# Two tiles of values moved beside the first scores, the first shift transposed half a step sooner

## The reference

```python
Q = (x @ Wq.T + bq).reshape(B, S, H, hd).transpose(0, 2, 1, 3)
K = (x @ Wk.T + bk).reshape(B, S, H, hd).transpose(0, 2, 1, 3)
V = (x @ Wv.T + bv).reshape(B, S, H, hd).transpose(0, 2, 1, 3)
scores = jnp.einsum('bhqd,bhkd->bhqk', Q, K) / (TAU * np.sqrt(hd))
A = jax.nn.softmax(scores, axis=-1)
A_stable = LAMBDA_JUMP * A + (1.0 - LAMBDA_JUMP) * L[None, None, :, :]
out = jnp.einsum('bhqk,bhkd->bhqd', A_stable, V)
out = out.transpose(0, 2, 1, 3).reshape(B, S, D)
return out @ Wo.T + bo
```

## Time and profile before

| | us |
|---|---|
| median of 3 runs | 2013.65 |
| lowest and highest run | 2012.37, 2017.76 |
| the profiled execution | 2025.48 |
| its span from first to last instruction | 2023.7 |
| PE busy | 1972.7 (97%) |
| DVE busy | 1621.5 (80%) |
| ACT busy | 1374.0 (68%) |
| mean granted clock of PE | 0.989 |

### The profile page before, as it was taken

One profiled execution on the slowest core, in us unless ns is written; L12 is line 12 of the kernel. 1 busy time (PEld: TensorE's weight loads), 2 busy tenths in 40 slices (PEclk: granted clock), 3 DMA queues, 4 the chain that ended last, 5 costly groups with the idle time before them and its releaser, 6 DMA issues. The chain is left out here.

```text
span 2023.7 us, 48037 instructions
## 1 busy us (share of the span) xinstructions
PE 1972.7 (97%) x16480; PEld 1051.8 (52%) x16480; DVE 1621.5 (80%) x2035; ACT 1374.0 (68%) x2471; POOL 347.4 (17%) x379
## 2 busy tenths in 40 slices
PE   7999999999999999999999999999999899999997
PEld 4543333333333333333333333333687689999996
DVE  6779999999999999999999999994255565555554
ACT  3338888888888888888888888889544422222331
POOL 1370001000100010001000100010024532232233
PEclk9979999999999999999999999999999899999999
DMA  7935335433543355335533553341122777788884
GB/s 268 243 81 114 74 84 118 91 73 79 121 93 73 76 112 105 73 74 107 112 73 74 105 114 73 73 97 49 42 76 87 286 228 238 241 256 302 256 267 111
DMA packets 105849, 264.09 MB, mean 130 GB/s; under 512 B 20896, under 2 KB 52768, under 8 KB 99104
## 3 DMA queue, kind: packets, MB, share of 16 engines
q1 hardware_dynamic: 92624, 245.29, 45.2%
q0 software_dynamic: 13152, 17.83, 4.5%
HBM read 206.95 MB, written 73.94 MB: 139 GB/s over the span
## 5 line engine op out<-in xcount | busy, mean ns | idle before, releaser
L619 DVE TENSOR_REDUCE part_max<-psum 128x1 f32<-128x1024 f32 x1024 | 1241.9, 1222 | 59.5 <-PE psum L741 47.0
L674 ACT ACTIVATE probs<-psum 128x512 f32<-128x512 f32 x2048 | 1111.1, 596 | 153.2 <-PE psum L754 86.1
L754 PE MATMUL psum<-score_q,score_k 50*128 50x512 f32 x2048 | 749.5, 448 | 1.2 <-DMA score_q<-shift_row 1.2
L741 PE MATMUL psum<-max_k,max_q 48*128 48x512 f32 x2048 | 742.4, 451 | 1.2 <-DVE part_max L619 1.1
L766 PE MATMUL psum<-probs,v_ones 128*32 128x256 f32 x8192 | 658.0, 393 | 9.4 <-ACT heads_sb L689 9.0
L754 PEld LDWEIGHTS psum<-score_q,score_k 50*128 50x128 f32 x2048 | 308.6, 186 | 408.6 <-ACT probs L674 394.0
L766 PEld LDWEIGHTS psum<-probs,v_ones 128*32 128x32 f32 x8192 | 162.5, 108 | 383.3 <-issue 200.8
L741 PEld LDWEIGHTS psum<-max_k,max_q 48*128 48x128 f32 x2048 | 296.0, 186 | 13.9 <-issue 7.5
L1159 ACT ACTIVATE x_sb<-psum,x_sb 128x512 f32<-128x512 f32 (+1 forms) x160 | 101.4, 635 | 260.0 <-PE psum L1520 253.4
L1539 PE MATMUL psum<-w,h_hi 128*128 128x256 f32 x1120 | 204.9, 280 | 0.6 <-issue 0.3
L1539 PEld LDWEIGHTS psum<-w,h_hi 128*128 128x128 f32 x1120 | 180.0, 189 | 11.6 <-issue 0.5
(11 more groups left out here) (179 smaller groups left out, 1367.7 us busy)
## 6 DMA issues: line engine op xcount, KB each, us to landing
w<-w_split SPq DMA_DIRECT2D x40, 2048.0 KB
max_q<-qk_pieces SPq DMA_DIRECT2D x192, 128.0 KB, 7.4
score_k<-qk_pieces SPq DMA_DIRECT2D x192, 128.0 KB, 4.6
xs<-in_pads SPq DMA_DIRECT2D x33, 528.0 KB, 5.9
qk_pieces<-pieces SPq DMA_DIRECT2D x32, 512.0 KB, 4.7
w_split<-w_pair SPq DMA_DIRECT2D x32, 512.0 KB, 6.6
max_k<-qk_pieces SPq DMA_DIRECT2D x192, 64.0 KB, 7.4
score_q<-qk_pieces SPq DMA_DIRECT2D x192, 64.0 KB, 2.2
```

Of the source, the lines that this page charges most:

```text
L619: nc.vector.tensor_reduce(part_max[:, t, p:p + 1], ps_m[p].rearrange("q b f -> q (b f)"), axis=AXIS.X, op=ALU.max).then_inc(m_read, 1)
L674: nc.scalar.activation(probs[kb % 2][:, chunk * BLOCK:(chunk + 1) * BLOCK], bank_of(at), ACT.Exp, scale=float(HD) ** -0.5).then_inc(exp_do ...
L741: last = nc.tensor.matmul(ps_m[p][:, h, :], max_q[u][rows, t * P:(t + 1) * P], max_k[u][rows, p * BLOCK:(p + 1) * BLOCK], start=True, stop ...
L754: nc.tensor.matmul(bank_of(at), score_k[u][rows, kb * P:(kb + 1) * P], score_q[u][rows, part * BLOCK:(part + 1) * BLOCK], start=True, stop ...
```

## The change

Six edits, all in the lead-in of `attend`:

- `v_tiles_before` spreads 28 instead of 30 tiles over halves 0 to 36, and puts tile 30 behind the score of half 38 and tile 31 behind that of half 39.
- The last bank, 15, is `ps_o` instead of `ps_s[1]` (`ps_v`). PE doesn't wait for an earlier bank ahead of it.
- At half 38 PE waits for 15 copied banks instead of 16. A wait for all 16 stands behind the lead-in, ahead of the heads' loop.
- SHIFT_HALF is 34 instead of 35; BANKS_BEFORE_SHIFT follows from the two, 13 instead of 15.
- ACT copies bank 15 between the second and third exponential of the first key block.
- `copy_v` is told its bank.

```diff
-    SHIFT_HALF = 2 * (ST + 1) + 1
+    SHIFT_HALF = 2 * (ST + 1)
...
-        return V_AHEAD + half * (TILES - V_AHEAD) // (FIRST_SCORES - 1) if half < FIRST_SCORES else TILES
+        spread = V_AHEAD + half * (TILES - 2 - V_AHEAD) // (FIRST_SCORES - 1)
+        return spread if half < FIRST_SCORES else min(TILES, TILES - 2 + half - FIRST_SCORES)
...
+    ps_v = [ps_s[r % VB] for r in range(BANKS - 1)] + [ps_o]
...
-        for r in range(BANKS_BEFORE_SHIFT // VB * VB, BANKS):
+                copy_v(b, vb, ps_s[vb])
+        for r in range(BANKS_BEFORE_SHIFT // VB * VB, BANKS - 1):
...
-            copy_v(r // VB, r % VB)
+            copy_v(r // VB, r % VB, ps_v[r])
         for c in range(CH):
             exp(0, 0, c, False)
+            if c == 1:
+                copy_v((BANKS - 1) // VB, (BANKS - 1) % VB, ps_o)
...
-            if t == 0 and r >= VB:
+            if t == 0 and VB <= r < BANKS - 1:
                 pe.wait_ge(v_copied, r - VB + 1)
...
-                last = nc.tensor.matmul(ps_s[vb][:, t * DIM:(t + 1) * DIM], xnT[:, b, k, toks], w_v[:, k, :],
+                last = nc.tensor.matmul(ps_v[r][:, t * DIM:(t + 1) * DIM], xnT[:, b, k, toks], w_v[:, k, :],
...
-                    pe.wait_ge(v_copied, BANKS)
+                    pe.wait_ge(v_copied, BANKS - 1)
...
+        pe.wait_ge(v_copied, BANKS)
```

More of the change, by code:

```diff
@@ L689, in copy_o, with copy_v @@
             nc.scalar.activation(heads_sb[:], ps_o, ACT.Copy).then_inc(o_copied, 1)
-        def copy_v(b, vb):
+        def copy_v(b, vb, bank):
             act.wait_ge(v_ready, VB * b + vb + 1)
-            nc.scalar.activation(v_tiles(b, vb), ps_s[vb].rearrange("p (t h d) -> p t h d", t=2, d=HD), ACT.Copy
+            nc.scalar.activation(v_tiles(b, vb), bank.rearrange("p (t h d) -> p t h d", t=2, d=HD), ACT.Copy
                                  ).then_inc(v_copied, 1)
@@ L698, in _ @@
             for vb in range(VB):
-                copy_v(b, vb)
-        for r in range(BANKS_BEFORE_SHIFT // VB * VB, BANKS):
+                copy_v(b, vb, ps_s[vb])
+        for r in range(BANKS_BEFORE_SHIFT // VB * VB, BANKS - 1):
             if r == BANKS_BEFORE_SHIFT:
```

## The result

The changed kernel is slower: 2026.64 us median of 18 runs (lowest 2018.38), against 2014.28 for the kernel before in the same job (lowest 2012.37). The ratio is 1.0062, with a 95% interval of 1.0040 to 1.0083. In a second job it was 2027.7 against 2014.39, ratio 1.0063 (1.0036 to 1.0090). The forecast was 2011.75, within 2002 to 2016. The profiled execution took 2030.82 us, with a span of 2029.0. One execution of each kernel in the first job was disturbed (2745.67 and 2302.79 us) and is left out of the ratio; without the two the medians are 2025.59 and 2013.97.

A forecast was written before the change was run, and what follows sets the result against it. PE was taken to bound the kernel, busy 97% of the span; 1.8 us by the maxima and 2.0 by the values were taken as 1.9 off 2013.65, giving 2011.75 us, range 2002 to 2016.

The forecast's parts named there:

- Steps 1 and 2: Lead-in: two tiles fewer ahead of half 37 take 2.12 us off PE; the earlier shift removes PE's 1.19 us wait.
- Step 3: Scores to heads' loop: maxima 42 start at 129.35, 1.8 us sooner; first values matmuls come 2.0 us sooner.
- Step 4: Wait for bank 15 ahead of the heads' loop costs nothing, 0.7 us cover; GpSimd's later pass is hidden.
- Step 2: Shift half a step sooner: lands at 124.0, PE wants it at 124.6; SP's entries behind it about 4 us sooner.
- The sum: Whole change: 1.8 us by the maxima and 2.0 by the values, taken as 1.9; bounds 0.7 and 2.4.
- The main doubt: Behind the lead-in: the median run before may well lack the profiled execution's low-clock stretch, which cost 9.1 us.
- Rival B: Lead-in: filling the gap also keeps the clock up, 1.9 + 9.1 = 11.0 us off, 2002.7 us; chance 0.21.
- A: Lead-in: idle time is filled, the median run's clock unchanged, 1.9 us off, 2011.75 us; chance 0.60.
- Rival D: Clock falls in the changed median run, for instance behind DVE's starving at 128: 7.2 us slower, 2020.9; chance 0.07.
- What would show it: Profile signs: PE busy over 4.3 of 5 us in 124 to 129; wrong if clock 0.50 within 130 to 150.

The follow-up runs named there:

- sp_after: The changed kernel, with SP issuing in each head the loads of the maxima's operands ahead of the weight chunk's store: 2008.11 us, ratio 0.9950 to the kernel before.
- sp_before: The kernel before, with SP issuing in each head the loads of the maxima's operands ahead of the weight chunk's store: 2013.46 us, ratio 0.9988.
- sp_after_again: The same kernel as sp_after, run once more in another job beside the changed kernel: 2007.56 us, ratio 0.9955 to the kernel before.
- pool_late_before: The kernel before with three more copies of the router weight's high part on POOL ahead of its long pass: 2028.41 us, ratio 1.0041.

## Why the prediction was wrong, point by point

- Steps 1 and 2, tiles and shift: right as to PE. PE reached half 37 at 123.59 (123.8 forecast), the transpose stood at 118.66 (119.2), the wait of 1.19 is gone.
- Step 3: right to 0.1 us at maxima 42 and the first values, so the gain of some 1.9 at that point is there (1.74 and 2.23).
- **Step 4 failed.** It said that POOL's lateness is hidden, since "The next thing wanted of it is the split of the second shift, at 168.68 now". The lateness was sized nearly right: some 1.5 us forecast, 1.67 measured at the start of the pass. Step 4 even reckoned POOL's work behind the pass, the first chunk's split among it, to an end near 153.7 (153.92 measured), but did not ask who waits for that split. SP's store does, and behind that store stand loads for which PE waits. Step 2 looked down SP's queue behind the shift and stopped at the first chunk's load; its "Nothing of PE's waits for these" is true of the band, the pads and that load, but the store and, two entries behind it, the loads that count come next. The sum put both the wait and its clock at nothing; in the profiled execution they were 8.1 us of wait and 14.5 us of low clock. Step 4's other claim, that the wait for bank 15 costs nothing, held.
- The question that was not asked is one of slack: how much sooner may PE come before it meets the loads? In the profiled execution before, PE came at 167.63 and the loads landed near 163.6 (165.39 less 1.84), so the slack was some 4.1 us. The changed kernel brought PE there at 157.2, 10.4 us sooner (the gain of the lead-in, and the 9.1 us that the clock no longer cost), and the loads 1.84 later. Together that is 12.3 us taken from 4.1, which leaves a wait of 8.2 us, and 8.1 were measured; the sum must come out, since the landing is read from the changed kernel's own trace. What it shows is that most of the slack was used up by the better clock and not by POOL. So every us that PE gains ahead of these loads is paid back as waiting once the slack is gone. I had asked what the faster clock does to POOL's shift (157.7 against an end at 153.7) and did not ask it of the DMAs.
- The main doubt, whether the median run before has a low stretch, was well placed. The answer is a short one, by estimate: in three later jobs 45 of 97 executions of the kernel before show a clock of 0.993 or 0.994 at some 2013 us, which is about 24 us at the low clock, against 16 in `sp_after`. The profiled execution, with 20 us at the low clock right behind the lead-in, was not typical.
- Rival B named the right mechanism in the lead-in: filling the gap keeps the clock up. Of 5.35 us between `sp_before` and `sp_after`, 1.9 is step 3's; the rest, 3.4, fits the shorter low stretch of `sp_before`, which by its rows costs 8.8 x (1 - 50/86.5) = 3.7 us, with 86.5 for the matmuls of 8.8 us at full clock. So A (1.9) and B (11.0) each held a part of it, but the loads took all of it away again.
- Rival D had the sign and the half clock, but with DVE's starving at 128 as the cause, and the price as 7.2. The trace shows 1.00 through there. What brought the clock down was a gap of 8.1 us that no rival held.
- "What would show it" listed a low clock within 130 to 150 and no stretch behind it, so it would have found nothing there.

What stays open is why the low stretch lasts 8 to 33 us behind the gap in one profile and another, and by the clocks of the unprofiled executions up to some 70. How the loss divides between wait and clock in the median execution is an estimate: the changed kernel's medians lie 18.5 and 20.1 us above those of `sp_after` and `sp_after_again`; some 8.2 of it is the wait, the other 10 to 12 the clock.

## What to carry to other kernels

Work that an engine hands over later is priced by everyone who waits for it, and a queue of DMAs hands the wait on: follow each wait on it to the entries behind, until one is found that the critical engine needs. When the critical engine gets faster, ask of every load that is timed by another engine whether it still lands in time. Put the loads that the critical engine needs ahead of stores that wait for a side job; here that order, or an earlier side job, turned a change that lost 12 us by the medians into one that gains 7.

## What the runs showed of the hardware

- In the lead-in the granted clock fell behind a stretch in which no single idle time of PE was over 1.4 us. In all six profiles without the whole change it fell between 128 and 131; PE had been busy there 3.55 to 3.65 of the 5.00 us from 124 on. In all seven with the whole change, busy 4.63 to 4.94 us in the same stretch, it held. A gap does not always do it: at 1582 in the kernel before PE was busy 0.63 of 2 us and the clock stayed at 1.00.
- Once down it stayed at 1.2 GHz for 32.9 us with PE busy 32.90 of them in the changed kernel, for 32 in `pool_late_before`, for about 10 in `sp_before`. The Trainium skill ("TensorE: Matmul & The Clock Gate", Part 1) says that activity releases the throttle. The clock did rise in all of these runs while PE was busy, but only after tens of us of it in some executions, and sooner in others.
- A low stretch costs less than its clock says: 181 matmuls against 323 in the same time, so 44% of the work is lost and not half. The line through the 28 executions gives 0.44 as well.
